# Cross attention over a short context: keys of four heads in three chunks of 104 rows instead of four of 77, with staggered rounds and the values' bias folded into the output bias

## What is computed

```
q = _split_heads(query @ Wq.T + bq)
k = _split_heads(key @ Wk.T + bk)
v = _split_heads(value @ Wv.T + bv)
scores = jnp.einsum('bhqd,bhkd->bhqk', q, k)
scores = scores * tau[:, :, None, None] + delta[:, None, None, :]
scores = scores / jnp.sqrt(jnp.asarray(DK, scores.dtype))
p_attn = jax.nn.softmax(scores, axis=-1)
x = jnp.einsum('bhqk,bhkd->bhqd', p_attn, v)
x = x.transpose(0, 2, 1, 3).reshape(query.shape[0], -1, H * DK)
return x @ Wo.T + bo
```

## Time and profile before

| | |
|---|---|
| median of 3 runs | 2463.38 us |
| lowest and highest run | 2454.69 and 2463.98 us |
| span of the profiled execution | 2453.9 us |
| PE busy | 2258.2 us, 92% |
| DVE busy | 1855.3 us, 76% |
| ACT busy | 1294.0 us, 53% |
| POOL busy | 1156.2 us, 47% |

### The profile page before, as it was taken

The page is one execution under the profiler, slowest core; times in us unless marked ns, Lnnn a source line. Parts: engine busy times, 40 slices in busy tenths (PEclk is TensorE's granted clock), DMA queues, the critical chain, the costliest instruction groups (busy, mean ns, idle before and its releaser), DMA issues.

```text
span 2453.9 us, 83619 instructions
## 1 busy us (share of the span) xinstructions
PE 2258.2 (92%) x36334; PEld 1535.8 (63%) x36430; DVE 1855.3 (76%) x4185; ACT 1294.0 (53%) x2400; POOL 1156.2 (47%) x856
## 2 busy tenths in 40 slices
PE   8999897878999999999999999999999999879985
PEld 4568553445666666766766666767667676645564
DVE  6732577779988889798988888897989888546612
ACT  3523253355666656666566666566665665325331
POOL 1036300046666556665656656665656655300064
PEclk8989898999999999999999999999999999879898
DMA  9012100010101211021111111121111110220012
GB/s 300 31 29 41 56 2 1 1 31 20 46 24 37 68 45 33 20 68 37 41 37 31 57 45 33 37 68 28 33 37 33 36 42 20 53 88 2 20 37 77
DMA packets 63736, 106.92 MB, mean 44 GB/s; under 512 B 11700, under 2 KB 48831, under 8 KB 56844
## 3 DMA queue, kind: packets, MB, share of 16 engines
q1 hardware_dynamic: 57626, 93.00, 13.4%
q0 software_dynamic: 4736, 8.29, 1.6%
q10 hardware_dynamic: 1010, 0.29, 0.1%
HBM read 42.55 MB, written 13.24 MB: 23 GB/s over the span
## 4 chain that ended last, share of the span: by engine, by line
PE 63%; DVE 12%; POOL 11%; issue 9%; ACT 3%; DMA 1%; POOLq 0%; SPq 0%; ACTq 0%; DVEq 0%
PE ps L2168 10%; PE ps L2271 6%; PE ps L2250 5%; POOL mem L2937 5%; PE ps L2212 4%; PE ps L2189 4%; PE ps L2177 4%; PE ps L2227 3%; POOL mem L2950 3%; PE ps L2330 3%; PE ps L2316 3%; PE ps L2307 2%; PE ps L1181 2%; PE ps L1662 2%; POOL mem L2944 2%
## 5 line engine op out<-in xcount | busy, mean ns | idle before, releaser
L2937 POOL TENSOR_TENSOR mem<-mem 128x512 f32<-128x512 f32 x384 | 571.6, 1496 | 547.9 <-DVE mem L2468 544.6
L2168 PE MATMUL ps<-mem 128*128 128x512 f32 x768 | 379.8, 606 | 9.5 <-DVE mem L2468 4.2
L2770 ACT ACTIVATE mem<-ps 128x512 f32<-128x512 f32 x384 | 221.4, 604 | 156.4 <-PE ps L2189 155.9
L2749 ACT ACTIVATE mem<-ps 128x512 f32<-128x512 f32 x384 | 220.7, 597 | 142.7 <-PE ps L2168 112.1
L2463 DVE TENSOR_TENSOR mem<-ps,mem 128x512 f32<-128x512 f32 x384 | 258.3, 673 | 12.7 <-ACT mem L2749 12.7
L2468 DVE TENSOR_TENSOR mem<-ps,mem 128x512 f32<-128x512 f32 x384 | 260.7, 679 | 0.0
L2189 PEld LDWEIGHTS ps<-mem 128*128 128x128 f32 x1536 | 182.4, 141 | 115.2 <-issue 95.2
L2250 PEld LDWEIGHTS ps<-mem 64*64 64x64 f32 x12288 | 192.8, 136 | 80.3 <-issue 78.4
L2475 DVE TENSOR_REDUCE mem<-mem 128x16 f32<-128x1024 f32 x192 | 231.7, 1207 | 0.0
L2950 POOL TENSOR_TENSOR mem<-mem 128x1024 f32<-128x1024 f32 x96 | 182.5, 1902 | 98.1 <-DVE mem L2535 98.1
L2189 PE MATMUL ps<-mem 128*128 128x128 f32 x1536 | 211.0, 273 | 5.9 <-DVE mem L2508 3.1
(11 more groups left out here) (307 smaller groups left out, 4135.1 us busy)
## 6 DMA issues: line engine op xcount, KB each, us to landing
mem<-mem SPq DMA_DIRECT2D x48, 768.0 KB, 5.8
mem<-in_Wqkv SPq DMA_DIRECT2D x6, 1536.0 KB, 6.6
mem<-mem SPq DMA_DIRECT2D x36, 256.0 KB, 3.5
y<-mem SPq DMA_DIRECT2D x8, 512.0 KB, 6.0
mem<-in_W12T SPq DMA_DIRECT2D x8, 512.0 KB, 7.7
mem<-y SPq DMA_DIRECT2D x16, 256.0 KB, 4.8
mem<-in_L3W SPq DMA_DIRECT2D x16, 256.0 KB, 5.6
mem<-in_L2Wo SPq DMA_DIRECT2D x6, 512.0 KB, 6.9
```

Of the source, the lines that this page charges most:

```text
L2168: e.matmul(self.K.ps[:, o, :], self.columns(u, bb), self.K.l2[l % 2]["Wqkv"][:, 512 * i:512 * i + 512], start=True, stop=True, skip_group_ ...
L2937: e.tensor_tensor(t1[:, cols], t1[:, cols], self.T2[:, cols], ALU.add).then_inc(s("rotated"), 1)
```

## The change

The four heads i of a row group have 4 x 77 = 308 columns in `kz`. Instead of four pieces of 77, one a head, they are now cut into three chunks of 104, 104 and 100 (`CHUNK`, `ROWS`), which cut through heads. A window has three chunks, NQ = 3 NW in all, and everything with keys on the partitions goes by them: the maxima's pattern `pick` (now 308 wide), the bias `deltaB`, the values `vz` (for each chunk, batch and head with the rows that don't belong to the head zeroed by the `heads` columns of a new constant `frames`), and the ones `oz`. `ctxT` is doubled in the second half (by a copy on POOL in the opening), so that a chunk of rows that runs over the end of the context can be read as one slice. Exponentials are six instructions of 104 x 512 a window instead of eight of 77 x 512.

The rounds are staggered: `pe_less(r)` does row groups 0 and 1 of chunk r and row groups 2 and 3 of chunk r - 1, so that the two heads sharing a bank are written in different rounds. `pe_weigh` takes one chunk. The values' bias no longer goes into the values: `pe_bias_row` multiplies it by Wo, ACT copies the row out, and POOL adds it to `bo` before `bo` is added to x.

```
+CHUNK, ROWS = 104, (104, 104, 100)
...
-    NQ = 2 * NW
+    NQ = 3 * NW
...
     def tensor(self, e):
         self.pe_turn_rows(e, 0)
+        if not self.early:
+            self.pe_values(e, 2)
         self.pe_queries(e, 0)
...
         for w in range(self.NW + 1):
-            if w < self.NW:
-                self.pe_less(e, 2 * w)
+            self.pe_less(e, 3 * w)
             if batch:
                 self.pe_turn_rows(e, w // 2 + 1)
             if next:
                 self.pe_score(e, w + 1, 2)
             if w >= 1:
-                self.pe_weigh(e, 2 * w - 1)
+                self.pe_weigh(e, 3 * w - 2)
             if batch:
                 self.pe_queries(e, w // 2 + 1)
             if next:
                 self.pe_score(e, w + 1, 3)
-            if w < self.NW:
-                self.pe_less(e, 2 * w + 1)
+            if this:
+                self.pe_less(e, 3 * w + 1)
+            if w >= 1:
+                self.pe_weigh(e, 3 * w - 1)
             if w >= 2:
                 self.pe_project(e, w - 2)
             if next2:
                 self.pe_score(e, w + 2, 0)
-            if w < self.NW:
-                self.pe_weigh(e, 2 * w)
+            if this:
+                self.pe_less(e, 3 * w + 2)
+                self.pe_weigh(e, 3 * w)
             if next:
                 self.pe_turn_max(e, w + 1)
...
+    def pe_values(self, e, c):
+        K, at, n = self.K, CHUNK * c % L, ROWS[c]
         for b in range(B):
-            o = ps[0:L, 6, 128 * b:128 * b + 128]
-            e.matmul(o, K.ctxT[:, b, :], w["Wv"], start=True, stop=False, skip_group_check=True)
-            last = e.matmul(o, K.onesf[0:1, 0:L], w["bv"][0:1], start=False, stop=True, skip_group_check=True)
+            last = e.matmul(K.ps[0:n, self.value_banks[c], 128 * b:128 * b + 128], K.ctxT[:, b, at:at + n], self.w["Wv"], start=True,
+                            stop=True, skip_group_check=True)
+    def pe_bias_row(self, e):
+        e.wait_ge(self.K.s["xo" + self.n], 32)
+        e.matmul(self.K.ps[:, 7, 384:512], bc(self.w["bv"][:, 0], 1, 128), self.w["Wo"], start=True, stop=True, skip_group_check=True)
...
+    def pe_less(self, e, r):
+        if r < self.NQ:
+            parts += [(r, 0), (r, 1)]
+        if r:
+            parts += [(r - 1, 2), (r - 1, 3)]
+        if r % 3 == 0 and r < self.NQ:
+            e.wait_ge(*s.at("max_cols", r // 3 + 1))
+        for p, j in parts:
+            w, c = divmod(p, 3)
+            if r >= 2 and j < 2:
+                e.wait_ge(*s.at("exped", 2 * (r - 2) + j + 1))
+            elif r == self.NQ:
+                e.wait_ge(*s.at("exped", 2 * (r - 2) + j - 1))
...
+    def cell(self, p, j):
+        return self.K.ps[0:ROWS[p % 3], 2 + 2 * (p % 2) + j % 2, 256 * (j // 2):256 * (j // 2) + 256]
...
     def gpsimd(self, e):
+        e.wait_ge(*s.at("bias_row", 1))
+        bo = self.w["bo"]
+        t = K.p(e.tensor_tensor(bo, bo, self.bvo, ALU.add))
...
     def p_start(self, e):
+        e.memset(self.vz[0:CHUNK], 0.0).then_inc(self.s("value_frame"), 1)
+        if self.opening:
+            e.wait_ge(*self.constants)
+            e.tensor_copy(K.ctxT[:, :, L:2 * L], K.ctxT[:, :, 0:L]).then_inc(K.s["first_cleared"], 1)
```

More of the change, by code:

```diff
@@ L446, in __init__ @@
             m.at = pt_where
-        self.pt = [tile4(4, 2, 256) for _ in range(3)]
+        self.pt = [tile4(2, 2, 256) for _ in range(3)]
         assert pt_where or m.at <= K.late - 1024
@@ L474, in tensor @@
         for w in range(self.NW + 1):
-            batch, next, next2 = w % 2 == 0 and w // 2 + 1 < B, w + 1 < self.NW, w + 2 < self.NW
-            if w < self.NW:
-                self.pe_less(e, 2 * w)
+            batch, this, next, next2 = w % 2 == 0 and w // 2 + 1 < B, w < self.NW, w + 1 < self.NW, w + 2 < self.NW
+            self.pe_less(e, 3 * w)
             if batch:
@@ L541, in pe_score @@
             e.wait_ge(*s.at("maxed", 1))
+        elif k and not self.early:
+            e.wait_ge(*self.values_of((2, 1)[k - 1]))
         for x in range(2):
@@ L566, in pe_turn_max @@
         last.then_inc(s("max_turn"), 1)
[L568 to L592, removed]
[L593 removed]
+    def pe_less(self, e, r):
+        K, s, parts = self.K, self.s, []
+        if r < self.NQ:
[10 more added lines that the diff above has]
+                e.wait_ge(*s.at("exped", 2 * (r - 2) + j - 1))
+            rows, keys, cols = slice(32 * j, 32 * j + 32), slice(CHUNK * c, CHUNK * c + ROWS[c]), slice(256 * (w % 2), 256 * (w % 2) + 256)
+            e.matmul(self.cell(p, j), view(self.kz[rows, w // 2], "p i l -> p (i l)")[:, keys], self.qT[rows, w // 2 % 2, cols],
+                     start=True, stop=False, skip_group_check=True)
+        for p, j in parts:
+            w, c = divmod(p, 3)
+            rows, keys = slice(32 * j, 32 * j + 32), slice(CHUNK * c, CHUNK * c + ROWS[c])
+            last = e.matmul(self.cell(p, j), K.pickb[rows, keys], self.mT[w % 2][rows, :], start=False, stop=True,
+                            skip_group_check=True)
+            if j >= 2:
+                last.then_inc(s("lessened"), 1)
@@ L607, in pe_weigh @@
+        for j in range(4):
+            h = 128 * b + 32 * j
+            e.matmul(K.ps[32 * j:32 * j + 32, 6, 0:256], self.vz[0:n, c, h:h + 32], pt[0:n, j % 2, j // 2, :], start=c == 0,
+                     stop=c == 2, skip_group_check=True)
+        for j in range(4):
+            last = e.matmul(K.ps[32 * j:32 * j + 32, 6, 256:512], self.oz[0:n, c, :], pt[0:n, j % 2, j // 2, :], start=False,
+                            stop=c == 2, skip_group_check=True)
         last.then_inc(s("weighed"), 1)
@@ L722, in v_start @@
             self.v_query_bias(e)
-        v(e.memset(self.oz[0:L], 0.0))
-        e.wait_ge(v.sem, v.n)
-        for i in range(4):
-            last = e.memset(self.oz[0:L, i, 8 * i:8 * i + 8], 1.0)
-        last.then_inc(s("value_frame"), 1)
+        if not self.opening:
+            self.v_ones(e)
         for r in range(2):
@@ L2119, in tensor @@
         self.pe_turn(e, f, 1)
-        after(e, freed[7])
-        after(e, freed[6])
+        for k in (7, 6, 2, 1):
+            after(e, freed[k])
         self.next.pe_start(e)
-        freed[7], freed[6] = [following.at("keys", 1)], [following.at("values", 4)]
+        freed[7] = [following.at("keys", 1)]
+        for c, k in enumerate(self.next.value_banks):
+            freed[k] = [self.next.values_of(c)]
         for bb in range(2):
```

168 lines of the change are left out of this document (96 added, 72 removed).

## The result

The changed kernel takes 2492.73 us (median of four runs, 2492.48 to 2501.21) against 2461.48 for the kernel before: 1.0146 of its time, 95% interval 1.0119 to 1.0172. It is slower by 31 us where the forecast was 4.6 us under the median then known, and it lies outside the forecast's range of 2440 to 2475. The profiled execution is the longest of the four (2501.21 us), 45.5 us of span above the one of before.

A forecast was written before the change was run, and what follows sets the result against it. VectorE was taken to end leg A, TensorE to bound leg B and, with exponentials, the last windows. Stages -12.3, fuller VectorE +0.4, starts +0.8 gave -11.1; clock falls +6.5 left -4.6 from median 2463.38: 2458.8 us, range 2440 to 2475.

The forecast's parts named there:

- two falls at 3.24 us: Clock halving at grown waits for rows or a maximum, each priced as one leg at half clock: +6.5 us together.
- the three places that it named: Third-window waits in the first two stages, growing to about 2 us, and the 361.22 wait, 1.48 to 2.4.
- low clock in the legs A: Rival: waits of 1.1 us or more in 15 legs A halve the clock; eight falls give 2478 us; chance 0.14.
- Leg A: Score 0 to score 2 of a window, 4.97 us, ended by VectorE: gain 0, TensorE's wait grows 0.23 to about 1.1.
- PE doesn't bound throughout: Denies the rival that TensorE bounds every window, each gaining 1.41 us, 33.8 in all: 2429.6 us; chance 0.14.
- a chunk grows by less than 104/77: Against the rival that chunk times grow with rows, to 0.82 and 1.32 us: 2462.7 without clock falls; chance 0.10.
- Leg B: Score 2 to the next score 0, bound by TensorE: 5.10 becomes 4.6 us, four a stage, -2.0 us.
- The last windows: End of a stage without scores, bound by TensorE and exponentials: 17.21 becomes 16.15 us, -1.05 a stage.
- the prediction's own bound of 1.73: Least time from score to score in a window: 0.87 + 0.80 + 0.06 us.
- The sum without the clock: Whole kernel: stages -12.3, fuller VectorE in the second stage +0.4, starts +0.8, together -11.1 us.
- The start: Opening of the first stage, shorter before the rows and five small VectorE steps fewer: -0.2 us.
- The bias row: Product of the values' bias with Wo in TensorE's queue ahead of the transposition, at half clock: +0.45 us a stage.

The follow-up runs named there:

- the pairs with the clock held: Changed kernel and kernel before, both with idle products at start and in legs: 2444.06 against 2451.90 us; both with ScalarE reciprocals and idle products: 2438.80 against 2446.36 us.
- full rounds: Changed kernel with all four row groups of a chunk scored together, each round waiting for both exponentials of the round before: 2526.04 us (1.0266).
- no bias row: Changed kernel without the product of the values' bias and Wo, its copy and its addition to bo: 2490.81 us.
- thin products: Changed kernel with four idle products over 3 rows of the array instead of 128 ahead of score 2 in leg A: 2489.35 us (1.0144).
- reciprocals alone: ScalarE instead of VectorE makes the reciprocals, without idle products: changed kernel 2439.52 us (0.9932), kernel before 2443.17 us (0.9933).
- maximum twice: Kernel before with the maximum that ends leg A computed twice in windows 2 to 7: 2494.90 us (1.0137).
- products in leg B: Changed kernel with four idle products ahead of score 0 in leg B, where TensorE does not wait: 2484.22 us.

## Why the prediction was wrong

**The step that failed is the clock.** It took two falls at 3.24 us, the price of one leg at half clock: +6.5 us. Two of the three places that it named did fall: the rows of the third window of attention 1 (at 343.75) for 3.4 us, and the score that stood at 361.22 (now 378.72) for 23.9. The third place lay in a stretch that was low already. On top came two long falls in ordinary legs A of attention 3 and a start in attention 0 that didn't recover, which the sum took at nothing. (The fall at 2260.4 stands at rows where the kernel before has its own.) The four long stretches held for 21 to 48 us each, and by the table they cost 11 us in attention 0, 9 at the end of attention 1 and 20 for the two of attention 3. The mistake was to read one short fall as the length of all. The rival "low clock in the legs A" had the right place and cause, the waits grown to 1.1 us. It also priced a fall at one leg, and so asked for eight where three long ones and the start's stretch were enough. The Trainium skill, "Perfetto Trace Analysis", Matmul Optimizations, asks for matmuls back to back in batches, since the engine scales its power with its use; the trace agrees at the falls, but from 380 to 404 PE is busy for 24.00 of 24.00 us at 0.51, so this alone didn't bring the clock back here. The same skill's "TensorE: Matmul & The Clock Gate", Part 1, tells of a kernel whose short idle spells between groups of matmuls made the clock go up and down; the five falls behind waits of 1.09 to 2.25 us agree.

**What was right.** Leg A is 4.97 us (71.11 to 76.08), to the hundredth what it was, and its wait is 1.08, forecast 1.1. That leg A gives 0 because DVE ends it holds. The grown wait in front of the rows came too (2.24, forecast about 2). The other rivals fell: PE doesn't bound throughout, and a chunk grows by less than 104/77.

**Sizes that were off.** Leg B is 4.70 (76.08 to 80.78): 0.40 shorter, forecast 0.5. The last windows of attention 0 at full clock, PE in order of time:

```profile
107.10 0.30 PE L572 MATMUL ps<-mem 3*128 3x308 bf16 x2 [1.33 <-DVE mem L803]
...
111.80 0.69 PE L613 MATMUL ps<-mem 32*100 32x256 f32 x8
...
112.53 0.64 PE L637 MATMUL ps<-mem 104*32 104x256 f32 x8
...
113.54 0.29 PE L593 MATMUL ps<-mem 128*128 128x128 bf16 x2
...
124.20 0.71 PE L658 MATMUL ps<-mem 128*128 128x128 f32 x4
```

They take 17.10 us, 0.11 less than the earlier trace rows, where 1.05 was forecast. A round of score chunks takes 0.73 (111.80 to 112.53) for the 0.61 I took, inside the bound of 0.82, and a weighing 1.01 for 0.98. The forecast spoke of six weigh and five score chunks less here; the timelines have 8 weigh chunks for 10 and 5.5 rounds of scores for 6. By these times that is some 1.0 us of PE work less (an estimate), not 2.8, and the waits take 0.9 of it back. The exponentials didn't grow: the pages have 684 ns for 104 rows and 679 for 77. A pair of them takes 1.26 us for the 1.20 of the forecast. The page after, then ACT in order of time:

```profile
L879 ACT ACTIVATE mem<-ps,mem 104x512 f32<-104x512 f32 x144 | 91.1, 684 | 119.2 <-PE ps L618 119.2
...
112.70 1.26 ACT L879 ACTIVATE mem<-ps,mem 104x512 f32<-104x512 f32 x2 [0.62 <-PE ps L618]
```

So a window loses 1.10 us of PE work (9.67 to 8.57 busy, above), not 1.41. Even with the reciprocals on ScalarE it is only 0.73 shorter (9.67 to 8.94): a wait of 0.37 is left ahead of score 2, since score to score takes 1.74 us (71.37 to 73.11), which is the prediction's own bound of 1.73. The sum without the clock was -11.1; the pairs with the clock held show -7.8, and -7.6 with runs that overlap.

**The start.** Forecast -0.2, 2.6 later in the profile. PE in order of time, start of attention 0:

```profile
10.01 0.76 PE L515 MATMUL ps<-mem 128*128 128x308 f32 x2 [3.78 <-DMA mem<-in_pick]
...
24.45 0.79 PE L533 MATMUL ps<-mem 128*128 128x128 f32 x2 [4.43 <-DVE mem L820]
25.04 0.42 PE L593 MATMUL ps<-mem 128*128 128x128 bf16 x2
...
31.16 1.11 PE L289 MATMUL ps<-mem 128*128 128x128 f32 x4 [1.93 <-DVE mem L265]
```

The wait for the first transfers is 3.78 us, before 0.33. But the first score stands at 14.88 to 17.37 us in the traces of the changed kernel and its variants, and at 14.81 to 19.63 in those of the kernel before: this varies from run to run, and the 2.6 can't be laid to the change. The bias row costs 0.59 (24.45 to 25.04) for 0.45.

**What stays open.** Why half-clock windows sometimes last: stretches of 44 us and more after a start came in 7 of the 15 attentions of five chunked kernels (changed, full rounds, no bias row, thin products, reciprocals alone), and in none of the 9 of three kernels with the old rounds (before, maximum twice, reciprocals alone; the longest there 30.7), in one profiled execution each. That is counted, not explained; nor is it shown why one wait of 1.1 to 1.3 us has a fall behind it and the next has none. Why products in leg B bring back only half wasn't tried further.

## What to carry to other kernels

Less work on TensorE, with another engine ending the leg, turns into a wait there, and the wait can cost the clock: price a fall by the whole stretch that it may last, not by one leg. Before cutting TensorE's work, shorten the chain that it waits for (here one reciprocal, 53 us in the changed kernel), or put full-size products into the wait. Compare variants also with the clock held in both; otherwise a gain of 8 us is hidden under a loss of 40.

## What was not expected of the hardware

TensorE busy without a pause, 24.00 of 24.00 us, stayed at 0.51. Products of 3 rows held the clock no better than none (2489 us), products of 128 rows and the same 1.0 us did (2449 us). Waits of 0.7 to 2.4 us in the legs of the kernel before, made by some 15 us of DVE work, cost 19 to 23 us beyond those 15. In that profile and the one of the changed kernel a fall came with all seven waits of 2 us and more, and with six of the seventeen of 1.05 to 1.52.
